# Placing k in its block diagonal by DMA instead of by copies, in the attention of a language-model block

## The reference

```python
h = base_weight[x] + lora_A.T[x] @ lora_B.T                 # 64 x 128 x 512
y = layernorm(h)
cq, ckv = layernorm(y @ W_dq)*g+b, layernorm(y @ W_dkv)*g+b # 128 columns each
Q, K, V = cq @ W_uq, *split(ckv @ W_ukv)                    # 512 columns each, 16 heads of 32
o = softmax(causal(Q K^T / sqrt(32))) V                     # per head
h = h + o @ W_o.T
h = h + ffn(layernorm(h))
```

## Time and profile before

| | us |
|---|---|
| median of 3 runs | 2719.15 (2715.58 to 2721.16) |
| the profiled execution | 2717.76 |
| its span in the trace | 2715.9 |
| PE busy over the span | 2541.1 (94%) |
| ACT busy | 1838.5 (68%) |
| DVE busy | 1724.4 (63%) |
| one turn of attention, from the stores of one group to those of the next (430.36, 498.68, 567.00) | 68.3 |

### The profile page before, as it was taken

The page is one execution under the profiler, slowest core; times in us unless marked ns, Lnnn a source line. Parts: engine busy times, 40 slices in busy tenths (PEclk is TensorE's granted clock), DMA queues, the critical chain, the costliest instruction groups (busy, mean ns, idle before and its releaser), DMA issues.

```text
span 2715.9 us, 49409 instructions
## 1 busy us (share of the span) xinstructions
PE 2541.1 (94%) x13120; PEld 1883.0 (69%) x13120; DVE 1724.4 (63%) x3742; ACT 1838.5 (68%) x4597; POOL 1126.7 (41%) x1275
## 2 busy tenths in 40 slices
PE   3899999999999999969999999999999999999999
PEld 2566666666666666547878777877877787787787
DVE  5666666666666666357656765765576576557655
ACT  2666666666666666557766866876686677668666
POOL 3433333333333333214444544544464454436445
PEclk8999999999999999979999999999999999999999
DMA  3121212121211111142221222122122213212221
GB/s 100 32 64 62 62 62 63 62 62 62 62 62 62 62 62 46 45 146 90 98 87 50 94 86 86 47 98 86 52 92 88 84 46 100 85 53 89 89 69 60
DMA packets 99807, 197.67 MB, mean 73 GB/s; under 512 B 10928, under 2 KB 10928, under 8 KB 99568
## 3 DMA queue, kind: packets, MB, share of 16 engines
q1 hardware_dynamic: 94576, 179.29, 19.6%
q0 software_dynamic: 5120, 17.31, 2.8%
HBM read 128.89 MB, written 34.08 MB: 60 GB/s over the span
## 4 chain that ended last, share of the span: by engine, by line
issue 28%; POOL 24%; PE 2%; DVE 1%; ACT 1%; POOLq 1%; DMA 0%; SPq 0%; DVEq 0%; ACTq 0%
POOL t_lo L1147 22%; POOL sh_lo L1147 1%; POOLq L1145 1%; DVE ps_u L1516 0%; DVE f_lo L1541 0%; ACT x L1310 0%; DVE t L1523 0%; DMA x<-h 0%; ACT t_hi L1365 0%; PE fwork L1162 0%; PE ps_g L1162 0%; PE ps_u L1164 0%; PE ps_g L1164 0%; PE ps_u L1162 0%; PE ps_y L1162 0%
## 5 line engine op out<-in xcount | busy, mean ns | idle before, releaser
L1147 POOL TENSOR_TENSOR t_lo<-t,t_hi 128x512 fp32r<-128x512 f32 x512 | 664.6, 1298 | 437.2 <-ACT t_hi L1365 437.1
L377 POOL TENSOR_TENSOR probs<-probs,inv 128x512 f32<-128x512 f32 x256 | 265.3, 1041 | 626.6 <-DVE inv L774 626.4
L599 ACT ACTIVATE probs<-ps_s,nmax 128x128 f32<-128x128 f32 x1024 | 363.6, 371 | 222.4 <-DVE nmax L769 222.3
L1516 DVE TENSOR_TENSOR ps_u<-ps_u,square 128x512 f32<-128x512 f32 x512 | 357.3, 698 | 179.5 <-ACT square L1352 142.2
L1365 ACT ACTIVATE t_hi<-t 128x512 fp32r<-128x512 f32 x512 | 320.8, 627 | 129.4 <-PE ps_y L1164 72.6
L1523 DVE TENSOR_TENSOR t<-ps_u,w_all 128x512 f32<-128x512 f32 x512 | 354.0, 691 | 54.2 <-DVE ps_u L1516 18.4
L1348 ACT ACTIVATE square<-ps_g 128x512 f32<-128x512 f32 x544 | 320.5, 589 | 91.7 <-PE ps_g L1164 89.6
L1352 ACT ACTIVATE square<-square 128x512 f32<-128x512 f32 x544 | 344.4, 633 | 17.3
L488 PE MATMUL ps_s<-k_diag,qT 128*128 128x512 f32 x512 | 264.0, 597 | 0.0
L769 DVE TENSOR_REDUCE nmax<-ps_s 128x4 f32<-128x512 f32 x256 | 176.1, 688 | 102.3 <-PE ps_s L488 100.8
L1162 PE MATMUL ps_y<-t_hi,f_hi 128*128 128x512 f32 x512 | 209.9, 410 | 21.9 <-POOL t_lo L1147 21.6
(11 more groups left out here) (196 smaller groups left out, 5519.5 us busy)
## 6 DMA issues: line engine op xcount, KB each, us to landing
w_all<-w_rows SPq DMA_DIRECT2D x256, 256.0 KB, 3.2
res_next<-h SPq DMA_DIRECT2D x64, 256.0 KB, 2.3
res<-res_next SPq DMA_DIRECT2D x64, 256.0 KB, 2.3
h<-res SPq DMA_DIRECT2D x64, 256.0 KB, 2.0
x<-h SPq DMA_DIRECT2D x16, 1024.0 KB, 5.8
fres<-h SPq DMA_DIRECT2D x16, 1024.0 KB, 7.7
out<-fres SPq DMA_DIRECT2D x64, 256.0 KB, 2.3
fres<-in_w_ffn SPq DMA_DIRECT2D x14, 512.0 KB, 3.6
```

What stands on the lines that cost most here:

```text
L377: pool.tensor_tensor(probs[:, s % 4, :, :], probs[:, s % 4, :, :], inv[:, s % 4, :].rearrange("p (h o) -> p h o", o=1).to_broadcast([P, HP ...
L599: e = act.activation(probs[:, s % 4, j, :], ps_s[:, s % 2, j, :], ACT.Exp, bias=nmax[:, s % 4, j:j + 1], accum_out=total[:, s % 4, j:j + 1])
L1147: pool.tensor_tensor(lo, t[:, t_slot(j), :], hi.bitcast(F32), ALU.subtract).then_inc(t_lo_done, 1)
L1516: dve.tensor_tensor(dst, product, square[:, j % 2, :], ALU.mult).then_inc(t1_done, 1)
```

## The change

Each chunk of k is copied out of PSUM in one instruction of 128 x 512, by ACT for chunks 0 and 2 and by DVE for chunks 1 and 3, to a new staging buffer `kT` with two slots (chunk i uses slot i % 2). When that copy is done, SP issues four DMAs (`place_k`), one per head, each from 32 rows of `kT` to the head's place in `k_diag`: 32 rows of four runs of 128 numbers (512 bytes), 64 KB. Four semaphores `k_placed` count them. PE now waits for `k_placed[m]` at steps 0, 4, 8 and 12 in place of the copies; ACT and DVE wait for the slot to be left before they copy. In SP's list chunks 1 and 2 stand ahead of the stores, chunk 3 ahead of the last store, chunk 0 at the end of the turn.

```diff
-ON_DVE = (("art", 1), ("q", 0), ("v", 1), ("v", 3))
-K_ON_DVE = (2, 3, 1, 2)
+ON_DVE = (("art", 1), ("q", 0), ("v", 1), ("v", 3), ("k", 1), ("k", 3))
...
+        kT = sb("kT", [P, 2, TOK], F32)
...
+        def k_slot_left(engine, n, i):
+
+            at_least(engine, k_placed[(i + 2) % DC], 16 * HPC * (n + (i != 1)))
...
+            def place_k(n, i):
+
+                if has_part(n, "k", i):
+                    bank, before = place(n, "k", i)
+                    wait_alone(sp, work_free[bank], DRAINS * (before + 1), sp_passed)
+                    for j in range(HPC):
+                        sp.dma_start(k_diag[j * DH:(j + 1) * DH, i, :, j, :],
+                                     kT[j * DH:(j + 1) * DH, i % 2, :].rearrange("p (t k) -> p t k", t=TILES)
+                                     ).then_inc(k_placed[i], 16)
+
             def turn(n):
+                place_k(n, 1)
+                place_k(n, 2)
                 if has_part(n, "out", 0):
                     for t in range(TILES):
+                        if t == TILES - 1:
+                            place_k(n, 3)
...
+                else:
+                    place_k(n, 3)
...
+                place_k(n, 0)
...
                     drained(pe, n - (m == 0), "q", m)
-                    drained(pe, n - (m == 0), "k", m)
+                    pe.wait_ge(k_placed[m], 16 * HPC * (n + 1))
...
             def k_copy(n, i):
-                if is_turn(n, -1):
-                    act.wait_ge(k_zeroed, 1)
-                for j in range(K_ON_DVE[i], HPC):
-                    op = act.activation(k_diag[j * DH:(j + 1) * DH, i, :, j, :],
-                                        bank_of(n, "k", i)[j * DH:(j + 1) * DH, :].rearrange("p (t k) -> p t k", t=TILES),
-                                        ACT.Copy)
-                was_read(op, n, "k", i, 1)
+                k_slot_left(act, n, i)
+                was_read(act.activation(kT[:, i % 2, :], bank_of(n, "k", i), ACT.Copy), n, "k", i)
...
             def k_copy(n, i):
-                full(dve, n, "k", i)
-                if is_turn(n, -1):
-                    dve.wait_ge(k_zeroed, 1)
-                for j in range(K_ON_DVE[i]):
-                    op = dve.tensor_copy(k_diag[j * DH:(j + 1) * DH, i, :, j, :],
-                                         bank_of(n, "k", i)[j * DH:(j + 1) * DH, :].rearrange("p (t k) -> p t k", t=TILES))
-                was_read(op, n, "k", i, 1)
+                k_slot_left(dve, n, i)
+                was_read(dve.tensor_copy(kT[:, i % 2, :], bank_of(n, "k", i)), n, "k", i)
```

More of the change, by code:

```diff
@@ L257, in attention_phase @@
         cT_done = sem("cT_done")
+        k_placed = [sem(f"k_placed{i}") for i in range(DC)]
         scores_full = sem("scores_full")
@@ L334, in turn @@
                         sp.dma_start(res_next[:, t, :], h[:, t, :]).then_inc(res_kept[t], 16)
+                place_k(n, 0)
+            sp.wait_ge(k_zeroed, 1)
             turn(-1)
@@ L783, in read_work @@
                     if has_part(n, part, i) and part in parts:
-                        if part == "k":
-                            k_copy(n, i)
-                        elif part == "out":
+                        if part == "out":
                             add_out(n, i)
@@ L795, in read_work @@
                                 q_copy(n, i)
+                            elif part == "k":
+                                k_copy(n, i)
                             else:
```

## The result

| | median us | runs |
|---|---|---|
| before, beside it | 2717.36 | 4 (2714.96 to 2721.16) |
| after | 2760.85 | 4 (2756.17 to 2762.77) |

The account below looks back on a forecast made before the run. PE's list was taken to bound attention. Chunk 0's wait 25.6 us, less 15 x 0.5 gained at step 1, plus 6.4 for the clock, made 24.5 us: 2743 us against a 2719.15 median, range 2726 to 2768.

Parts of the forecast that it names:

- Which wait, and where: PE's scores at step 0 wait about 2.1 us for chunk 0's placement, once per turn and at no other step.
- the wait for `ar`: PE's 1.36 us wait behind the row maxima stays, so it does not absorb the new wait at step 0; gain 0.
- chunk 3 is in time: Tightest of the three later chunks: copy ends at 516.2, placed at 520.0, wanted by PE at 523.27.
- `xn` and the exponentials: PE's waits of 1.46 us at step 5 and 0.59 us do not hang on k copies; gain 0.
- The placement: From end of copy to PE: 0.23 reaction, 3 x 0.46 issues, 2.1 landing, 0.1 to PE, 3.8 us; ends 3.3 and 4.7.
- The 0.50 for pT: Step 0: PE's wait for ACT's pT copy goes, scores ready at 534.40 instead of 534.90, but no gain.
- The 0.5 at step 1: Step 0 to 1: one DVE k copy instead of three lets PE go on sooner; gain 0.5 us per turn.
- The clock: PE's clock falls behind the new gap in one turn of two, 0.8 us each: 6.4 us, ends 0 and 16.
- Feed-forward is untouched, and I take its time as it is: The feed-forward part keeps its time; no term for it in the sum.
- Hidden: Rival: chunk 0 lands before 534.40, PE gains 1.0 us per turn, 15 us, 2704; chance 0.05.
- cancelled: Rival: a 2.6 us placement costs 0.4 per turn against a gain of 0.5; 2719 us; chance 0.06.
- much longer placements: Rival: small pieces or four transfers one after another take 8.4 us; 137 us slower, 2855; chance 0.06.

Follow-up runs that it names:

- e1: Changed kernel with chunk 0 of k copied straight into its block diagonal by ACT and DVE, chunks 1 to 3 still placed by DMA; 2709.27 us, ratio 0.9958.
- e3: Kernel before with only chunk 0 of k changed: one ACT copy to staging and four DMAs by SP; 2791.02 us, ratio 1.0262.
- e5: Changed kernel with chunk 0 of k made at the end of step 13 instead of midway in step 14; 2699.27 us, ratio 0.9933.
- e11: e1 with chunk 0 of k made at the end of step 13 and DVE's program padded; 2716.73 us, ratio 0.9995.
- e2: Changed kernel with nine matmuls without use on PE ahead of the wait for chunk 0; 2726.74 us, ratio 1.0032.
- e6: Changed kernel with 14 unread semaphore increments at the start of DVE's list, making its program 13 instructions longer; 2772.17 us.
- e4: Changed kernel with heads 0 and 1 of chunk 0 copied in place by DVE, the others placed by two DMAs; 2721.79 us, ratio 1.0017.
- e10: e1 with 57 unread semaphore increments, DVE's program 64 instructions longer than in the changed kernel; 2692.77 us, ratio 0.9905.
- e12: Changed kernel with four matmuls without use on PE ahead of the wait for chunk 0; 2728.91 us, ratio 1.0041.
- e9: Kernel before with 116 unread semaphore increments, DVE's program 128 instructions longer than in the changed kernel; 2706.53 us.

## Why the prediction was right or wrong

**Which wait, and where.** Right: chunk 0 alone (e1, e3), once per turn, not covered by the wait for `ar` behind it; chunk 3 is in time, issued from 536.29 on for scores that start at 543.12; `xn` and the exponentials gained nothing from the lighter copies.

**The placement.** Forecast 3.8 us from the end of the copy, measured 4.26. Landing 2.1, as taken. The issue was the mis-sized part: 0.68 from start to start against 0.46, above even the upper end of 0.67. I had taken it from loads with one run per partition; these transfers have four runs at the destination, and one issue takes 0.60 at the median, against 0.43 for those loads and 0.465 for `res_next<-h`, which stays within SBUF with one run. That the four runs are the reason was not tried. SP's reaction was 0.10 instead of 0.23. The wait of 2.27 against 2.1 came out closer than its parts.

**The 0.50 for pT.** It did not all go. PE's transposes start 3.00 us behind the scores ahead of them (550.38 to 553.38) where unhindered they would start about 0.2 earlier, and 3.43 before: something else ends their wait. POOL's product is the candidate, since e5 and e11 show that wait grown, but in the changed kernel the trace names no releaser here. So PE reached the wait 0.14 later than I had it (4.01 us behind the scores of step 15, not 3.87), which shortens the wait but not the turn. The step from scores to scores grew by 1.91 (6.28 against 4.37), not 1.6, for another reason: the placement took 0.46 longer, and ACT's copy ended 0.15 sooner (2.02 us behind those scores, where I had 2.17).

**The 0.5 at step 1.** Right: 2.83 from scores to start before (538.43 to 541.26), 2.35 after, and e1, where little else differs, has turns of 67.8 against 68.3.

**The clock.** The mechanism was named, the size was wrong: 6.4 us forecast, with 16 as the upper end, 31.8 measured by e2. I gave it one turn in two and 0.8 us each; it was 13 in 15 and 2.1 over all turns. Two errors: the gap of 2.1 us was nearer in effect to the 2.48 than to the 1.46 I had set beside it, and I priced every fall by the one example of the earlier trace rows, which was short (3.4 us low in the trace). The seven short falls cost 1.0 us each, near my 0.8; the other six, low for up to 17 us with PE at work, cost 1.7 to 6.2 and make up most of the loss.

**The sum.** Placement and gains 18.1 us forecast (25.6 - 7.5), 22.3 measured; clock 6.4 and 31.8; feed-forward 0 and -12.8. "Feed-forward is untouched, and I take its time as it is" is the step that failed outright: its code was untouched, its place was not. Without that the changed kernel would stand at 2772 (e6), outside the range. That the total fell inside the range is luck: it owes some 12 us to a gain that I had put at nothing.

**The rivals.** Hidden, cancelled and much longer placements are all out by the 2.27 us. The prediction set the 2.3 us landing of `res<-res_next` beside the 0.67 us between issues of `res_next<-h`; the latter land after 2.3 us too, so the argument stands. The rule that transfers to parts of the partitions serialize, from the Trainium skill, "DMA: Bandwidth & Descriptors", in "Rules for kernel authors", read as one whole transfer after another, is not what these traces show: the four are issued 0.68 apart and land 2.1 after the issue each. What the splitting costs here is the time per issue (e4); one transfer for all four heads was not tried.

## What to carry to other kernels

A handful of small DMAs costs their issues one by one plus one landing, 4.3 us here for four; where the reader comes in 2 us the copies that they save are worth nothing, and where it comes later they are free (e5). A wait on a busy TensorE costs more than its length, because the clock may fall behind it; idle slots filled with matmuls without use gave back 32 of 54 us. And two programs that differ in one phase may differ in another by the place of a loop: pad to the same place before a difference under half a percent is believed.

## What was not expected of the hardware

- DVE's feed-forward loop takes 1.0 us more per turn, 12 us in all, at some places of its program, with 65 more packets in the instruction queue (91 against 26). It comes round after 64 instructions (e10). That the packets are the cause of the 1.0 us was not tried apart from the place. At +5 (e3) the stall at the same point is another 1.1 us longer, with the same 91 packets, and that is not explained.
- The clock of TensorE fell behind gaps of 2.27 us in 13 of 15 turns and stayed at half for 3.4 to 17 us. It fell in none of 15 turns with gaps left of 1.3 or 1.1 (e12, e4), in four of 14 of e11 whose gap is 1.62, and in one turn of e9 with the gaps of the kernel before. In e2, with 0.2 left, it never fell. What sets the long stretches stays open.
- The 46 executions of the kernel before beside the experiments spread with their mean clock: those with 0.989 took 2713.7 to 2715.0 us, those with 0.984 took 2721.7 to 2725.4. Its clock may well fall in a turn or two of the slower ones, as in e9; only the means were kept, so this is not shown.
- An issue on SP of a 64 KB transfer within SBUF, with four runs of 512 bytes per partition, takes 0.60 us, against 0.43 for the loads of the weights at the start and 0.465 for 256 KB within SBUF in runs of 2 KB.
